# First feed-forward pass of a four-layer kernel: its weights loaded on ScalarE's queue into eleven tiles, split by ScalarE and VectorE; stacks cleared on Pool

## The chip, the cores and the metric

The kernel runs on one core of one Trainium2 chip. Its time is the device time of one execution in microseconds. Several executions are measured, and the median is given; one further execution is profiled. Engines are called TensorE (PE in the profile; PEld is its loading of weights), VectorE (DVE), ScalarE (ACT), Pool (GpSimd, POOL) and SyncE (SP), which issues the transfers.

## The reference, cut to what matters

The program is one chain of four blocks over x of shape (4, 1024, 128), each block a half feed-forward, a mixer and the half feed-forward again. The change touches the first line only:

```python
def _layernorm(x, axis=-1, eps=1e-05):
    m = jnp.mean(x, axis=axis, keepdims=True)
    v = jnp.var(x, axis=axis, keepdims=True)
    return (x - m) / jnp.sqrt(v + eps)
...
    def _L0_ffn_ref(x, w1_w, w1_s, w2_w, w2_s, h1_w, h1_s, h2_w, h2_s, w3_w, w3_s):
        ...
        def _tlin(x, w, s):
            return jnp.einsum('bsi,oi->bso', x, w) * s
        h = jax.nn.silu(_tlin(x, w1_w, w1_s)) * _tlin(x, w2_w, w2_s)
        h = jax.nn.gelu(_tlin(h, h1_w, h1_s), approximate=False)
        h = jax.nn.gelu(_tlin(h, h2_w, h2_s), approximate=False)
        return _tlin(h, w3_w, w3_s)
...
    x = x + 0.5 * _L0_ffn_ref(_layernorm(x, axis=-1), L0_ffn_w1_w, ..., L0_ffn_w3_s)
    x = x + _L0_attn_ref(_layernorm(x, axis=-1), ...)
    x = x + 0.5 * _L0_ffn_ref(_layernorm(x, axis=-1), L0_ffn_w1_w, ..., L0_ffn_w3_s)
    x = x + 0.5 * _L1_ffn_ref(...)
    ...
```

The feed-forward has 128 inputs and 512 hidden features; its weights are 128 x 5632 numbers as the kernel holds them. Attention, two kinds of Mamba mixer, mixtures of experts and a linear attention follow.

## The kernel before

**Layout.** The 4096 tokens stay in SBUF in `x_res`, features on the partitions, as eight chunks of 512 tokens. A feed-forward pass runs over the chunks i = 0 to 7. Products that must be exact to float32 are made of rounded parts: a matrix is split into a high part (rounded to the type fp32r) and a low part (what is left), and `split_mm` (L240 to L243) does three matmuls, high by high, low by high and high by low.

**Order of the work.** Every piece of work is a small generator, such as `dve_stage` or `pe_ffn_gated`, that yields a planned time ahead of each step. `weave` (L86) merges the generators of one engine by these planned times into one fixed list of instructions. On the chip an engine goes through its list in order and stops wherever it has to wait for a semaphore; the planned times set the order and nothing else. `T_FFN` is the planned start of the first hidden layer; all later plans are sums on it.

**The start.** SyncE loads the constants (`sp_setup`, nine transfers, L269 to L277), the chunks of x, and the weights of the first feed-forward in eleven pieces of 128 x 512 through the two tiles of `weight_staging` (`sp_stage`, L464). VectorE (`dve_setup`) waits for all constants, makes the router's two parts and bfloat16 copies, and raises `const_ready`; TensorE, ScalarE and Pool wait for that ahead of their first work. `dve_stage` makes each piece's high part by a cast (L473) and its low part by a subtraction (L475), and frees the staging tile. `dve_attn_setup` clears the stacks of the attention (L771 to L775); SyncE (`sp_attn_setup`) then writes rows of ones into them (L767).

**A chunk.** Its norm: four transposes on TensorE (L355), statistics on VectorE (L364 to L371), a power on Pool (L380), flattening on VectorE (L391), transposes back (L401), the high part on ScalarE (L411) and the low part on VectorE (L428). Four gates follow (f = 0 to 3): two products into PSUM (TensorE, L241 to L243), tanh (ScalarE, L550), two combining steps (VectorE, L559 and L563), high part (ScalarE, L576), low part (VectorE, L585). Then eight hidden tiles (o = 0 to 7): twelve matmuls each, two Gelus on ScalarE (L627, L628) and a low part on VectorE (L637); a last product and the sum into x. The low part of the weights is waited for by count (`wl_lo`): two pieces for the gates, six for the first hidden layer, ten for the second, eleven for the last product.

```python
    T_FFN = 42.0
    w0_count = stage_weights(3.0, 2.4, lambda: (), in_pieces(w0r, w0, L0W_COLS))
...
    on_dve += [dve_attn_setup, dve_ring, dve_found]
```

## Time and profile before

| | us |
|---|---|
| median of 3 runs | 3579.4 (3575.9 to 3581.34) |
| the profiled execution | 3582.58 |
| its span, first to last instruction | 3580.7 |
| TensorE busy | 3103.5 (87%) |
| VectorE busy | 2532.0 (71%) |
| ScalarE busy | 1999.0 (56%) |
| Pool busy | 660.5 (18%) |

The profile is one execution recorded by the hardware. Its page lists the busy time of each engine and of groups of instructions. Its rows name an engine, a line of the kernel, the operation and what it writes and reads. Behind a row or a group stands the idle time of the engine just before it and, after an arrow, what ended it. PEclk is the clock that TensorE was granted, as a share of full speed. SPq rows are transfers that SyncE issues; their time is that of issuing.

### The profile page before, as it was taken

The numbers are of one execution on the slowest core, as the hardware profiler recorded it, in microseconds if no ns is written. First come the engines' busy times: TensorE is split into PE (matmuls) and PEld (weight loads), VectorE is DVE, ScalarE is ACT, GpSimd is POOL, SyncE is SP. The second block draws the span as 40 slices with busy tenths as digits, with TensorE's granted clock in tenths as the row PEclk, the third lists the DMA queues.
The fourth block names the chain that finished last, engine by engine and source line by source line (L and its number), as shares of the span: only waits on it lengthen the run. The fifth ranks groups of instructions, "written<-read, shape, count | busy, mean of one in ns | idle before, by whom it ended". The sixth has DMA issues, their size and how long they took to land. (4 is left out here: it accounts for less than half of the span.)

```text
span 3580.7 us, 45680 instructions
## 1 busy us (share of the span) xinstructions
PE 3103.5 (87%) x15362; PEld 1927.4 (54%) x15362; DVE 2532.0 (71%) x5665; ACT 1999.0 (56%) x3483; POOL 660.5 (18%) x543
## 2 busy tenths in 40 slices
PE   4998888888999997689887777778899999799998
PEld 3776344343677663256543333334467776667776
DVE  5566677774554776778666888876677777667776
ACT  2443566667444444544435565643367777367776
POOL 0011101100000000000003444430023333023332
PEclk8999899999999998889998898889999999799999
DMA  2000122211100330023330000002421010011111
GB/s 83 1 10 28 45 60 64 66 56 35 42 1 1 111 101 2 0 69 97 106 108 27 1 0 1 1 18 86 136 66 43 29 48 27 1 45 42 30 48 51
DMA packets 99184, 159.65 MB, mean 45 GB/s; under 512 B 16220, under 2 KB 28956, under 8 KB 98824
## 3 DMA queue, kind: packets, MB, share of 16 engines
q1 hardware_dynamic: 98952, 156.74, 14.5%
q8 instruction: 123, 2.02, 0.2%
q14 instruction: 109, 0.89, 0.1%
HBM read 138.67 MB, written 17.99 MB: 44 GB/s over the span
## 5 line engine op out<-in xcount | busy, mean ns | idle before, releaser
L380 POOL TENSOR_TENSOR norm_rstd<-norm_rstd,minus_half 128x4 f32<-128x4 f32 x144 | 176.4, 1225 | 1594.3 <-DVE norm_rstd L371 1591.9
L2301 ACT ACTIVATE main_tiles_r<-banks,feature_cols 128x512 fp32r<-128x512 f32 x512 | 352.8, 689 | 188.5 <-PE banks L243 166.7
L2309 DVE TENSOR_TENSOR main_tiles_r<-main_tiles,main_tiles_r 128x512 fp32r<-128x512 f32 x512 | 382.7, 763 | 68.3 <-ACT main_tiles L2302 66.8
L862 DVE TENSOR_REDUCE gate_scratch<-banks 128x2 f32<-128x1024 f32 (+2 forms) x320 | 349.9, 1114 | 106.5 <-PE banks L812 62.7
L241 PE MATMUL banks<-normed_pairs,moe_weights 128*128 128x512 f32 x800 | 407.2, 509 | 13.9 <-ACT main_tiles L2302 6.5
L1010 ACT ACTIVATE main_tiles<-banks 128x512 f32<-128x512 f32 (+3 forms) x768 | 327.3, 497 | 163.2 <-PE banks L232 94.3
L2302 ACT ACTIVATE main_tiles<-banks,feature_cols 128x512 f32<-128x512 f32 x512 | 350.0, 684 | 0.0
L242 PE MATMUL banks<-normed_pairs,moe_weights 128*128 128x512 f32 x800 | 317.4, 397 | 0.0
L243 PE MATMUL banks<-normed_pairs,moe_weights 128*128 128x512 f32 x800 | 317.2, 397 | 0.0
L2346 POOL TENSOR_TENSOR normed<-normed,main_tiles 128x512 f32<-128x512 f32 x128 | 217.6, 1700 | 535.3 <-DVE main_tiles L2335 535.3
L241 PE MATMUL banks<-main_tiles_r,moe_weights 128*128 128x512 f32 x640 | 267.3, 418 | 29.4 <-DVE main_tiles_r L2309 26.9
L243 PE MATMUL banks<-main_tiles_r,moe_weights 128*128 128x512 f32 x640 | 250.9, 392 | 0.0
L242 PE MATMUL banks<-main_tiles_r,moe_weights 128*128 128x512 f32 x640 | 250.6, 392 | 0.0
L241 PE MATMUL banks<-main_tiles_r,ffn_weights 128*128 128x512 f32 x560 | 227.8, 407 | 10.9 <-DVE main_tiles_r L585 6.8
L241 PEld LDWEIGHTS banks<-normed_pairs,moe_weights 128*128 128x128 f32 x800 | 152.6, 191 | 135.9 <-ACT main_tiles L2302 48.9
L243 PE MATMUL banks<-main_tiles_r,ffn_weights 128*128 128x512 f32 x560 | 222.3, 397 | 0.0
L242 PE MATMUL banks<-main_tiles_r,ffn_weights 128*128 128x512 f32 x560 | 222.1, 397 | 0.0
L391 DVE TENSOR_SCALAR norm_flat<-banks,norm_means,norm_rstd 128x128 f32<-128x128 f32 x576 | 195.2, 401 | 29.6 <-POOL norm_rstd L380 29.5
L994 PE MATMUL banks<-q_stacks,k_stacks 64*128 64x512 bf16 (+3 forms) x768 | 179.6, 335 | 39.2 <-ACT main_tiles L1010 37.2
L401 PE MATMUL banks<-const_mats,norm_flat 128*128 128x128 f32 x576 | 104.9, 311 | 103.8 <-DVE norm_flat L391 103.3
L2215 POOL TENSOR_TENSOR mamba_tiles<-mamba_tiles 128x512 f32<-128x512 f32 x128 | 167.3, 1307 | 148.3 <-DVE mamba_tiles L2183 93.6
L364 DVE BATCH_NORM_STATS2 norm_stats<-banks 128x6 f32<-128x128 f32 x576 | 126.9, 282 | 79.0 <-PE banks L355 78.6
(347 smaller groups left out, 6850.0 us busy)
## 6 DMA issues: line engine op xcount, KB each, us to landing
main_tiles<-gates_d SPq DMA_DIRECT2D x400, 256.0 KB, 3.4
weight_staging<-in_w SPq DMA_DIRECT2D x33, 256.0 KB, 3.8
found_d<-main_tiles SPq DMA_DIRECT2D x32, 256.0 KB, 2.0
parts_d<-bf_parts SPq DMA_DIRECT2D x48, 128.0 KB, 1.8
q_stacks<-parts_d SPq DMA_DIRECT2D x192, 32.0 KB
k_stacks<-parts_d SPq DMA_DIRECT2D x192, 32.0 KB
x_res<-in_x_t SPq DMA_DIRECT2D x8, 256.0 KB, 3.4
weight_staging<-found_d SPq DMA_DIRECT2D x8, 256.0 KB, 3.5
```

The lines of the kernel that those rows point to most:

```text
L241: eng.matmul(o, wh, hi, start=first, stop=False)
L242: eng.matmul(o, wl, hi, start=False, stop=False)
L243: return eng.matmul(o, wh, lo, start=False, stop=last)
L380: eng.tensor_tensor(rstd[:, k, 1, :], rstd[:, k, 0, :], minus_half[:, :], ALU.pow).then_inc(s.norm_pow)
L391: z = eng.tensor_scalar(flat[:, k, sl], psum[:, b, sl], means[:, k, t, 0:1], rstd[:, k, 1, t:t + 1], ALU.subtract, ALU.mult)
L862: eng.tensor_reduce(o.rearrange("p (n s) -> p s n", s=2)[:, :, j0:j0 + per], psum[:, b0:b0 + 2, 0:per * (k1 - k0)].rearrange("p s (n c) -> ...
L994: z = eng.matmul(o[:, 0:C - q0], k_of(g, h, i * TILE, (i + 1) * TILE), q_of(g, h, half * C + q0, half * C + C), start=True, stop=not diag, ...
L1010: eng.activation(weight_tile(e)[:, 0:C - q0], psum[:, score_at[e], 0:C - q0], ACT.Exp, scale=HD ** -0.5).then_inc(s.at_exp)
L2301: eng.activation(pair_3(j)[0], psum[:, 2 + j % 2, :], ACT.Relu, bias=bias)
L2302: eng.activation(h3_of(j), psum[:, 2 + j % 2, :], ACT.Relu, bias=bias).then_inc(s.m3_h)
L2309: eng.tensor_tensor(lo, h3_of(j), hi.bitcast(F32), ALU.subtract).then_inc(s.m3_lo)
L2346: eng.tensor_tensor(total, total, gt_of(m3_u(k)), ALU.add).then_inc(s.moe_add)
```

## The change

The first pass no longer goes through the staging tiles. ScalarE issues the eleven loads ahead of everything else, into eleven tiles of `attn3_tiles`, a region that is used much later (the stacks of the attention overlay it). ScalarE makes the high parts with a Copy activation and VectorE the low parts. Four semaphores group the tiles by two, four, four and one. The clearing of the stacks goes to Pool and waits for all low parts, as it shares the place. SyncE issues chunk 0 and the identity first, and TensorE's first transposes wait for these two only (`mats_in`). VectorE's router block stands later. The chunks 2 to 7 share three semaphores, two by two. `T_FFN` goes from 42 to 27. Lines of the changed kernel: transposes L358, statistics L367 to L374, power L383, flattening L394, transposes back L404, norm's high and low part L414 and L431, weights' high and low part L511 and L517, tanh L588, gate steps L597 and L601, gate's high and low part L614 and L623.

```diff
-    x_ready = [lambda c=c: (x_in[c], 16) for c in range(NC_)]
+    x_ready = [lambda c=c: (x_in[c], 16 if c < 2 else 32) for c in range(NC_)]
...
     def sp_setup(eng):
         yield 0.0
+        eng.dma_start(chunk(0), x_t[:, 0:C]).then_inc(x_in[0], 16)
+        eng.dma_start(matf[:, :], mats[:, 0:KEPT_MATS]).then_inc(s.mats_in, 16)
         eng.dma_start(colv[:, :], cols).then_inc(s.const_in, 16)
+        eng.dma_start(chunk(1), x_t[:, C:2 * C]).then_inc(x_in[1], 16)
         eng.dma_start(rowv[:, :], rows).then_inc(s.const_in, 16)
-        eng.dma_start(matf[:, :], mats[:, 0:KEPT_MATS]).then_inc(s.const_in, 16)
...
-        for c in range(NC_):
-            yield 0.1 + (0 if c < 2 else 8 + c)
+        for c in range(2, NC_):
+            yield 16.0 + 8 * (c // 2)
...
     def dve_setup(eng):
...
-        yield 1.0
-        eng.wait_ge(s.const_in, 144)
-        for kind, ne in (("l1", 8), ("l2", 9), ("l3", 8)):
-            w = RW[kind]
-            eng.tensor_copy(routerr[:, 2 * w:2 * w + ne], routerw[:, w:w + ne]).then_inc(s.const_ready)
+        yield 5.5
+        eng.wait_ge(s.mats_in, 16)
+        eng.wait_ge(s.const_in, 128)
         eng.tensor_copy(matb[:, 0:P], ident)
...
+        yield 40.0
         for kind, ne in (("l1", 8), ("l2", 9), ("l3", 8)):
...
     def pe_setup(eng):
         yield 0.0
-        eng.wait_ge(s.const_ready, 6)
...
+        eng.wait_ge(s.mats_in, 16)
+        yield 60.0
+        eng.wait_ge(s.const_ready, 7)
...
-    T_FFN = 42.0
-    w0_count = stage_weights(3.0, 2.4, lambda: (), in_pieces(w0r, w0, L0W_COLS))
+    T_FFN = 27.0
+    w0_pieces = in_pieces(w0r, w0, L0W_COLS)
...
+    def w0_group(k):
+
+        return (0, 2) if k < 2 else (1, 4) if k < 6 else (2, 4) if k < 10 else (3, 1)
+
+    def act_w0_in(eng):
+        yield 0.0
+        for k, (_, src) in enumerate(w0_pieces):
+            eng.dma_start(w0_tile(k), src).then_inc(w0_in[w0_group(k)[0]], 16)
+
+    def w0_at(k):
+        return 6.0 + 1.5 * k
+
+    def act_w0_hi(eng):
+        for k, (dst, _) in enumerate(w0_pieces):
+            yield w0_at(k)
+            n, count = w0_group(k)
+            eng.wait_ge(w0_in[n], 16 * count)
+            eng.activation(dst[:, 0, :], w0_tile(k), ACT.Copy).then_inc(s.w0_hi)
+
+    def dve_w0_lo(eng):
+        for k, (dst, _) in enumerate(w0_pieces):
+            yield w0_at(k) + 0.8
+            eng.wait_ge(s.w0_hi, k + 1)
+            eng.tensor_tensor(dst[:, 1, :], w0_tile(k), dst[:, 0, :].bitcast(F32), ALU.subtract).then_inc(s.w0_lo)
...
     def sp_attn_setup(eng):
-        yield 20.0
+        yield 60.0
...
-    def dve_attn_setup(eng):
-        yield 12.0
+    def pool_attn_clear(eng):
+        yield 34.0
         eng.memset(fin_ones, 1.0)
+        eng.wait_ge(s.w0_lo, len(w0_pieces))
         eng.memset(ks_t.bitcast(F32)[:, :, :, :], 0.0)
-        yield 18.0
+        yield 40.0
         eng.memset(qs_t.bitcast(F32)[:, :, :, :], 0.0)
         eng.memset(v_t[:, :, :], 1.0).then_inc(s.at_set)
```

VectorE's list before, from the low part of the first norm (L428) on; `weight_staging` holds a piece of weights, `ffn_weights` its two parts, and L559, the first gate's combining step, stands nineteen rows below the last one shown:

```order
L428 TENSOR_TENSOR normed_pairs<-banks,normed_pairs 128x512 [waits norm_out]
L473 CAST ffn_weights<-weight_staging 128x512 [waits wl_in0]
L475 TENSOR_TENSOR ffn_weights<-weight_staging,ffn_weights 128x512 [waits wl_hi]
L771 MEMSET gate_scratch 128x1024
L772 MEMSET k_stacks 128x6144
L473 CAST ffn_weights<-weight_staging 128x512 [waits wl_in1]
L475 TENSOR_TENSOR ffn_weights<-weight_staging,ffn_weights 128x512 [waits wl_hi]
L473 CAST ffn_weights<-weight_staging 128x512 [waits wl_in0]
L475 TENSOR_TENSOR ffn_weights<-weight_staging,ffn_weights 128x512 [waits wl_hi]
L774 MEMSET q_stacks 128x3072
L775 MEMSET v_rows 128x1408
L473 CAST ffn_weights<-weight_staging 128x512 [waits wl_in1]
```

VectorE's list in the changed kernel, from behind the flattening of the first norm to the combining step of the first gate (L597):

```order
L517 TENSOR_TENSOR ffn_weights<-attn_tiles,ffn_weights 128x512 [waits w0_hi] x3
L431 TENSOR_TENSOR normed_pairs<-banks,normed_pairs 128x512 [waits norm_out]
L517 TENSOR_TENSOR ffn_weights<-attn_tiles,ffn_weights 128x512 [waits w0_hi]
L367 BN_STATS norm_stats<-banks 128x6 [waits norm_in]
L367 BN_STATS norm_stats<-banks 128x6 x3
L371 BN_AGGR norm_means<-norm_stats 128x2 [waits norm_stat]
L371 BN_AGGR norm_means<-norm_stats 128x2 x3
L374 TENSOR_SCALAR norm_rstd<-norm_means 128x4 [waits norm_mean]
L517 TENSOR_TENSOR ffn_weights<-attn_tiles,ffn_weights 128x512 [waits w0_hi] x3
L394 TENSOR_SCALAR norm_flat<-banks,norm_means,norm_rstd 128x128 [waits norm_pow]
L394 TENSOR_SCALAR norm_flat<-banks,norm_means,norm_rstd 128x128 x3
L597 SCALAR_TENSOR_TENSOR spare_nat<-spare_nat,banks 128x512 [waits ffn_tanh]
```

The clearing and the casts are gone from between the two, and seven of the eleven subtractions are left there. Right behind it, VectorE's list of the changed kernel in the first two gates:

```order
L601 SCALAR_TENSOR_TENSOR spare_nat<-banks,half_s_and_half_s_s_63,spare_nat 128x512 [waits ffn_mid,ffn_gt]
L517 TENSOR_TENSOR ffn_weights<-attn_tiles,ffn_weights 128x512 [waits w0_hi] x2
L623 TENSOR_TENSOR main_tiles_r<-spare_nat,main_tiles_r 128x512 [waits ffn_ghi]
L431 TENSOR_TENSOR normed_pairs<-banks,normed_pairs 128x512 [waits norm_out]
L597 SCALAR_TENSOR_TENSOR spare_nat<-spare_nat,banks 128x512 [waits ffn_tanh]
L601 SCALAR_TENSOR_TENSOR spare_nat<-banks,half_s_and_half_s_s_63,spare_nat 128x512 [waits ffn_mid,ffn_gt]
L517 TENSOR_TENSOR ffn_weights<-attn_tiles,ffn_weights 128x512 [waits w0_hi] x2
L623 TENSOR_TENSOR main_tiles_r<-spare_nat,main_tiles_r 128x512 [waits ffn_ghi]
```

Four subtractions stand in the gates, where before none stood. ScalarE's list before, from its start:

```order
L411 ACT_TABLE_LOAD [waits norm_back]
L411 ACTIVATE normed_pairs<-banks 128x512 [waits const_ready]
L550 ACTIVATE spare_nat<-banks,half_s_and_half_s_s_63 128x512 [waits ffn_up]
L576 ACTIVATE main_tiles_r<-spare_nat 128x512 [waits ffn_g]
L411 ACTIVATE normed_pairs<-banks 128x512 [waits norm_back]
```

And now; `attn_tiles` is where the eleven pieces land:

```order
L501 DMA attn_tiles<-in_w 128x512 x11
L511 ACT_TABLE_LOAD
L511 ACTIVATE ffn_weights<-attn_tiles 128x512 [waits w0_in0] x2
L414 ACTIVATE normed_pairs<-banks 128x512 [waits norm_back]
L511 ACTIVATE ffn_weights<-attn_tiles 128x512 [waits w0_in1] x4
L511 ACTIVATE ffn_weights<-attn_tiles 128x512 [waits w0_in2]
L588 ACTIVATE spare_nat<-banks,half_s_and_half_s_s_63 128x512 [waits const_ready,ffn_up]
L511 ACTIVATE ffn_weights<-attn_tiles 128x512 [waits w0_in2] x2
L614 ACTIVATE main_tiles_r<-spare_nat 128x512 [waits ffn_g]
```

The table load stands ahead of the first copy and no longer behind the first norm; a copy of the third group (`w0_in2`) stands ahead of the first tanh (L588). TensorE's list keeps its order but for two places some hundreds of microseconds later, where two neighbours change places.

## Rows read from the trace of the kernel before

**Rows 1.** Waits, 0 to 80 us: who waited for whom, us in total, times, longest

```profile
ACT main_tiles_r L576 <- DVE spare_nat L563: 34.4, 4, 29.3
...
DVE ffn_weights L473 <- DMA weight_staging<-in_w: 6.4, 3, 4.3
```

**Rows 2.** Order of time, VectorE, 21 to 50 us: start us, us, engine, line, operation

```profile
21.48 5.18 DVE L772 MEMSET k_stacks<- 128x6144 f32 x1 [1.23 <-issue]
...
42.77 0.43 DVE L473 CAST ffn_weights<-weight_staging 128x512 fp32r<-128x512 f32 x1 [4.33 <-DMA weight_staging<-in_w]
...
49.02 0.68 DVE L559 SCALAR_TENSOR_TENSOR spare_nat<-spare_nat,banks 128x512 f32<-128x512 f32 x1
```

**Rows 3.** Order of time, 7 to 21 us, constants to the first tanh

```profile
7.37 0.32 DVE L292 CAST router_w_r<-router_w 128x8 fp32r<-128x8 f32 x3 [6.29 <-DMA main_tiles<-in_mats]
...
8.35 0.31 DVE L301 TENSOR_TENSOR router_w_r<-router_w,router_w_r 128x8 fp32r<-128x8 f32 x3
...
8.99 1.11 PE L355 MATMUL banks<-const_mats,x_res 128*128 128x128 f32 x4 [8.99 <-DVE half_s_and_half_s_s L306]
...
11.80 1.05 POOL L380 TENSOR_TENSOR norm_rstd<-norm_rstd,minus_half 128x4 f32<-128x4 f32 x1 [11.36 <-DVE norm_rstd L371]
...
12.88 1.36 DVE L391 TENSOR_SCALAR norm_flat<-banks,norm_means,norm_rstd 128x128 f32<-128x128 f32 x4 [0.18 <-POOL norm_rstd L380]
...
15.50 1.28 ACT L411 ACT_TABLE_LOAD   x1 [15.50 <-PE banks L401]
...
17.42 0.69 DVE L428 TENSOR_TENSOR normed_pairs<-banks,normed_pairs 128x512 fp32r<-128x512 f32 x1 [2.12 <-ACT normed_pairs L411]
...
18.17 1.12 PE L355 MATMUL banks<-const_mats,x_res 128*128 128x128 f32 x4 [2.75 <-DVE normed_pairs L428]
...
20.60 0.69 ACT L550 ACTIVATE spare_nat<-banks,half_s_and_half_s_s 128x512 f32<-128x512 f32 x1 [3.21 <-PE banks L243]
```

**Rows 4.** Stretch 20 to 48 us: length, busy us by engine, PEclk, DMA share, GB/s

```profile
20.00:48.00 28.00, 1.85 (x5) 0.93 (x3) 19.18 (x30) 0.69 (x1) 1.12 (x1) 0.59 0.43 146
```

**Rows 5.** Order of time, a gate's low part and the first hidden matmul

```profile
54.73 0.69 DVE L585 TENSOR_TENSOR main_tiles_r<-spare_nat,main_tiles_r 128x512 fp32r<-128x512 f32 x1 [0.70 <-ACT main_tiles_r L576]
...
61.19 0.50 PE L241 MATMUL banks<-main_tiles_r,ffn_weights 128*128 128x512 f32 x1 [3.28 <-DVE main_tiles_r L585]
```

**Rows 6.** Order of time, SyncE's issues of the last constant and of chunks 0, 1

```profile
4.96 0.60 SPq L277 DMA_DIRECT2D main_tiles<-in_mats  x1
5.60 1.06 SPq L280 DMA_DIRECT2D x_res<-in_x_t  x2
```

**Rows 7.** Stretches of 3 us, columns as in rows 4

```profile
6.00:9.00 3.00, 0.01 (x1) 0.02 (x1) 1.52 (x13) 0.00 (x0) 0.00 (x0) 1.00 0.79 195
...
36.00:39.00 3.00, 0.00 (x0) 0.00 (x0) 1.12 (x2) 0.00 (x0) 0.00 (x0) 0.50 1.02 410
```

**Rows 8.** Groups, 0 to 62 us: line, engine, shapes, count, busy us, mean ns, idle before

```profile
L475 DVE TENSOR_TENSOR ffn_weights<-weight_staging,ffn_weights 128x512 fp32r<-128x512 f32 x11 | 7.6, 692 | 0.4
...
L576 ACT ACTIVATE main_tiles_r<-spare_nat 128x512 fp32r<-128x512 f32 x4 | 2.5, 630 | 34.4 <-DVE spare_nat L563 34.4
```

**Rows 9.** Order of time, TensorE at the sixth gate's first product

```profile
76.69 0.50 PE L241 MATMUL banks<-normed_pairs,ffn_weights 128*128 128x512 f32 x1 [1.32 <-DVE spare_nat L559]
```

**Rows 10.** Groups, Pool, whole run: its memset of the odd v rows

```profile
L1096 POOL MEMSET v_rows_odd<- 128x1408 f32 x1 | 1.3, 1271 | 0.0
```

**Rows 11.** TensorE's clock: a stretch (columns as in rows 4), the page's 40 slices

```profile
62.00:66.10 4.10, 4.10 (x13) 3.19 (x12) 0.00 (x0) 0.64 (x2) 0.00 (x0) 0.58 0.00 0
...
PEclk8999899999999998889998898889999999799999
```

**Rows 12.** Order of time, Pool and VectorE subtract at once, 250 to 253 us

```profile
250.75 1.66 POOL L887 TENSOR_TENSOR spare_nat<-spare_nat 128x512 f32<-128x512 f32 x1 [1.73 <-DVE spare_nat L839]
251.19 1.77 DVE L637 TENSOR_TENSOR main_tiles_r<-spare_a,main_tiles_r 128x512 fp32r<-128x512 f32 x1
```

More of the change, by code:

```diff
@@ L482, in build, with w0_tile @@
     FFN_US = 31.0
-    T_FFN = 42.0
-    w0_count = stage_weights(3.0, 2.4, lambda: (), in_pieces(w0r, w0, L0W_COLS))
+    T_FFN = 27.0
+    w0_pieces = in_pieces(w0r, w0, L0W_COLS)
+    def w0_tile(k):
+        return wb_t[:, k, :]
+    def w0_group(k):
[17 more added lines that the diff above has]
+            eng.tensor_tensor(dst[:, 1, :], w0_tile(k), dst[:, 0, :].bitcast(F32), ALU.subtract).then_inc(s.w0_lo)
+    on_act += [act_w0_in, act_w0_hi]
+    on_dve.append(dve_w0_lo)
     ffn_b = [T_FFN + FFN_US * i for i in range(NC_)]
@@ L529, in pe_ffn_gated @@
                 if i == 0 and f == 0:
-                    eng.wait_ge(s.wl_lo, 2)
+                    eng.wait_ge(s.w0_lo, 2)
                 if q == 32:
@@ L547, in act_ffn_tanh @@
                 eng.wait_ge(s.ffn_up, q + 1)
+                if q == 0:
+                    eng.wait_ge(s.const_ready, 3)
                 if q >= 2:
```

47 lines of the change are left out of this document (24 added, 23 removed).

## The prediction

> **What bounds the kernel now.** I read the list of waits of the first 80 us first, since every edit of the change lies there. The reader is to see one wait that is out of proportion: ScalarE's rounding of the first gate tile (L576) waits 34.4 us for VectorE in four times, 29.3 us of it in one, while the weights' own transfers cost VectorE only 6.4 us [rows 1]. Next VectorE's part of the order of time. The tanh of the first gate is started at 20.60, so its tile is ready at 21.3, but VectorE takes it up (L559) only at 49.02. In between stand, in one in-order queue, the clearing of the k stacks (5.18 us in one instruction), of the q stacks and v rows, eight of the eleven weight splits, some of which wait for a transfer (4.33 us at 42.77), and the second norm [rows 2, 3]. The table of stretches gives the whole gap: from 20 to 48 us VectorE is busy for 19.18 us of 28, TensorE for 1.85 [rows 4]. So the first gate of the first feed-forward pass, and with it all that TensorE has to do later, waits for VectorE's queue, and not for data. From 61 us on the kernel runs as a chain of semaphores in which TensorE is busy for most of the time, and nothing in it goes by the clock on the wall: what is won before the first hidden layer (first matmul at 61.19) [rows 5] is won for the end, unless something gives it back.
>
> **The change, part by part: the start.** What stays on the path are the constants, the norms of chunk 0 and 1, the splits that stand ahead of the first gate, and the four gates. I rebuild the times from rows.
> 1. TensorE now waits for chunk 0 and the identity only, SyncE's first two transfers. Before, its first transposes waited for all constants and start at 8.99 [rows 3]. They can now start at about 6 (0.6 MB and as much of weights, 3 us at the fast rate, after those 2.5), but VectorE does its constant casts ahead of the flattening (L394 of the new kernel), and these still wait for the last constant. Call that landing T. Before it ends the wait at 7.37; SyncE's last constant was issued from 4.96 to 5.56, so it took 1.8 us more [rows 3, 6]. SyncE now issues two chunks ahead of it at 0.53 us each (1.06 for two) [rows 6], which puts T at 8.4 at the earliest. At the latest: SyncE's list up to there is 1.4 MB (two chunks 0.5, the matrices 0.35 and 0.2, the rest small), and ScalarE's queue may bring as much again of weights beside it. 2.8 MB at the slow row's 195 GB/s are 14.4 us, at the fast row's 410 GB/s 6.8 us, and some 2.5 us from the first issue to the first landing come on top: 17 or 9.3 [rows 7]. The slow stretch held the many small constants, and what is added are pieces of 256 KB, so I stay near the fast end: **T = 10.5**, with 8.4 and 17 as ends.
> 2. VectorE's constant block takes 1.6 us before (7.37 to 8.99); its six router instructions, 0.32 and 0.31 us [rows 3], go to a later place. It ends at T + 1.0 = 11.5. The first norm's power is done by then (2.8 us from the transposes to Pool's start, and 1.05 us: 6 + 3.9 = 9.9) [rows 3].
> 3. From flattening to the paired residue (L428) it was 12.88 to 17.42, 4.54 us, with a table load of 1.28 in it [rows 3]. The table load now stands ahead of ScalarE's weight copies, beside the transfers: 3.2 us are left. New in between are one weight copy on ScalarE and one subtraction on VectorE (the third tile's; order section), 0.63 and 0.69 us [rows 8]. L428's work starts at 11.5 + 3.2 + 1.3 = 16.0.
> 4. The second transposes follow 0.75 us later (18.17 against 17.42), the tanh 2.4 us after these (20.60), Pool's power 2.8 us after them and 1.05 us long [rows 3]: 16.8, 19.2, 19.6 to 20.7. VectorE does three more subtractions (2.1 us) from 19.6, then the flattening of 1.36 us [rows 3, 8], and takes up the first gate at **23.0 where it was 49.02**.
> 5. The four gates took 61.19 − 49.02 = 12.17 us before [rows 2, 5]. Four subtractions of 0.69 now stand in them, two and two, each pair in a gap in which VectorE waited 0.70 us for ScalarE's rounding [rows 5, 8]: + 2 × (1.38 − 0.70) = 1.4. First hidden matmul at 23.0 + 12.2 + 1.4 = **36.5 where it was 61.19**. Gained: 24.7.
>
> **What moves behind it.** The router block (1.0 us with its semaphore) now stands between VectorE's fourth hidden residue and the fifth gate, where TensorE already waits 1.32 us for VectorE [rows 9]: − 1.0, and 0 if it is hidden. ScalarE's eleven casts cost 11 × 0.63 = 6.9 us [rows 8] in a stretch in which it waited 34 us [rows 1]; its eleven DMA issues some 5 us by SyncE's 0.53, over at about 6 and ahead of anything it must do. Eleven casts (L473) leave VectorE. The clearing goes to Pool, at 0.90 ns an element by Pool's own memset (1271 ns for 1408) [rows 10]: k stacks 5.5, q stacks 2.8, v rows 1.3, together 9.6 us, begun when the last split is done, at about 29. It is over by 39; Pool's next power was needed at 83 and is now needed at 59, and the stacks are wanted only by the attention, hundreds of microseconds later. So it costs nothing unless it holds VectorE (first rival). SyncE loses nine waits on staging and issues chunks 2 to 7, the rope table and the attention weights at once. The rest of the program keeps its order but for two places on TensorE where neighbours change; I put these at nothing. The two staging tiles change their turn only.
>
> **The sum.** 24.7 − 1.0 = 23.7 us. The profiled execution took 3582.58 (span 3580.7, 1.9 around it), so it would be 3558.9. That execution lay 3.2 above the median of the runs, 3579.4, so I forecast **3555.7**.
>
> **What would speed it up.** T at 8.4 (−2.1), the four subtractions hidden (−1.4), the router block hidden (−1.0), and the slow piece of the first hidden layer gone: 62 to 66.1 has a granted clock of 0.58, between the levels 1.2 and 2.4 GHz, so 42% of 4.1 us, 1.7, were lost [rows 11]. Together −6.2: 3549.5.
>
> **Rivals.**
> *Transfers come late.* For it: 5.2 MB (ten weight tiles, and as much on SyncE's list) are wanted by about 20 us, and the stretch 6 to 9 moved 195 GB/s at a busy share of 0.79 [rows 7]. Against: 36 to 39 moved 410 GB/s from SyncE's queue alone. Price: T at 17 is + 6.5. ScalarE's seventh copy needs tiles 6 to 9 by 20.2 (one copy of 0.63 ahead of the third subtraction after 19.6) and stands ahead of the tanh; 5.2 MB at 410 GB/s are there at 15, at 195 GB/s at 29.2, + 9, and the two do not add. 3559 to 3565.
> The Trainium skill (DMA: Bandwidth & Descriptors, Issuing engines are not separate DMA queues) speaks against the change here: starting DMAs from several engines saves only the time of issuing. By it the second queue brings no bandwidth and T lies between 9.3 and 17; if the queues' rates added up, T would be 8.4. No row of this case has two queues at once.
> *Pool's clearing holds VectorE.* For it: while Pool subtracts at 250.75 (1.66 us), VectorE's subtraction with two SBUF inputs takes 1.77 us in place of 0.69 [rows 8, 12]. If a memset did the same, the residues of the second and third gate would stand behind 5.5 us, then 2.8 and 1.3: + 5 to + 9.6, 3561 to 3565. Against: that Pool instruction reads SBUF, a memset only writes; the row shows no such case.
> The Trainium skill (SBUF — State Buffer, Who interferes with whom) says that a VectorE instruction with two SBUF inputs contends with a GpSimd one that reads SBUF, not with one that only writes. By that the price is 0, by the row's slowdown carried over up to 9.6; no run here shows it yet.
> *The clock takes it back: slower than before.* The profile shows TensorE at a lowered clock after a stretch with gaps: 0.58 at 62 to 66.1, and the page's row of the clock has 11 slices of 40 below 9 tenths, spread over the run [rows 11]. All of them fall anew when the work starts 24 us earlier. At half clock and full work a microsecond costs half of one: to lose the 23.7 and 7.2 more (0.2%) the run needs 62 us more of half clock, fifteen pieces like that one. From there on it is slower, 3587. Against: the three runs before differ by 5.4 us in all, though their pieces fell as they liked. Taking back half of that spread is likely, all of the gain is not.
> *The change does not move the wait.* VectorE would still reach the first gate behind its queue. The order section excludes it: seven subtractions stand ahead of it, no memset and no wait on a staging tile.
>
> **Chances.** The forecast (3550 to 3559) 0.68, late transfers 0.15, Pool holding VectorE 0.07, more gain than 3549.5 0.04, the clock taking most or all back 0.04, no move 0.02. The range 3549 to 3565 holds the first three and leaves out about 1 in 10. About 0.2%, 7.2 us, is what a measurement of this kernel can tell from no change. Faster by more: 0.95; within it: 0.03; slower by more: 0.02.
>
> **What the new profile would show.** Right: VectorE's first gate step at 22 to 24 and the first hidden matmul at 35 to 38; the wait of ScalarE's rounding for VectorE down from 29.3 to a few us; Pool's memsets from 29 to 39 with VectorE's subtractions at 0.69 beside them; all later landmarks some 24 us earlier up to the end. Wrong: VectorE's constant casts starting after 13 (late transfers); a subtraction of 2 us or more beside a memset (Pool); the hidden layer 24 us earlier but the end less than 18 (the clock, or a wait that I have not seen behind the first pass).

## The result, and the profile after

The changed kernel takes 3559.44 us (median of four runs, 3552.9 to 3562.62) against 3580.37 of the kernel before (3575.9 to 3583.12): a ratio of 0.994 with a 95% interval of 0.9922 to 0.9958, 15 to 28 us. Forecast were 3555.7 in a range of 3549 to 3565. The profiled execution took 3557.94 (span 3555.8). In a second series of the same kernel (first experiment below) the ratio is 0.9931, interval 0.9914 to 0.9948.

First the waits of the first 60 us, which answer to [rows 1] (who waited for whom, us in total, times, longest). ScalarE's rounding of the gates (now L614) waited 34.4 us for VectorE before; one wait of 29.3 is gone. VectorE's wait for the last constant, 6.29 us at the very start before [rows 3], now stands behind the statistics of the first norm, from 8.87 to 14.16.

```profile
ACT main_tiles_r L614 <- DVE spare_nat L601: 9.1, 5, 3.1
...
DVE const_mats_bf L294 <- DMA main_tiles<-in_mats: 5.3, 1, 5.3
```

The order of time from the first transposes to the fifth gate, which answers to [rows 2, 3, 5, 9] (start us, us, engine, line, operation). The landmarks are the constant casts (L294), the flattening (L394), the paired residue (L431), the first tanh (L588), VectorE's first gate step (L597), and TensorE at the first hidden matmul and at the matmul of [rows 9], which waits for VectorE's first step of the fifth gate; below it stands for "the fifth gate".

```profile
6.20 1.11 PE L358 MATMUL banks<-const_mats,x_res 128*128 128x128 f32 x4 [6.20 <-DMA const_mats<-in_mats]
...
9.02 1.01 POOL L383 TENSOR_TENSOR norm_rstd<-norm_rstd,minus_half 128x4 f32<-128x4 f32 x1 [8.57 <-DVE norm_rstd L374]
...
14.16 0.23 DVE L294 CAST const_mats_bf<-const_mats 128x128 bf16<-128x128 f32 x1 [5.29 <-DMA main_tiles<-in_mats]
...
15.18 1.36 DVE L394 TENSOR_SCALAR norm_flat<-banks,norm_means,norm_rstd 128x128 f32<-128x128 f32 x4
...
19.51 0.68 DVE L431 TENSOR_TENSOR normed_pairs<-banks,normed_pairs 128x512 fp32r<-128x512 f32 x1
...
22.68 0.69 ACT L588 ACTIVATE spare_nat<-banks,half_s_and_half_s_s 128x512 f32<-128x512 f32 x1 [1.74 <-PE banks L244]
...
25.90 0.68 DVE L597 SCALAR_TENSOR_TENSOR spare_nat<-spare_nat,banks 128x512 f32<-128x512 f32 x1
...
32.56 5.23 POOL L811 MEMSET k_stacks<- 128x6144 f32 x1 [7.29 <-DVE ffn_weights L517]
...
35.66 0.69 DVE L623 TENSOR_TENSOR main_tiles_r<-spare_nat,main_tiles_r 128x512 fp32r<-128x512 f32 x1 [0.70 <-ACT main_tiles_r L614]
...
39.25 0.80 PE L242 MATMUL banks<-main_tiles_r,ffn_weights 128*128 128x512 f32 x1 [3.27 <-DVE main_tiles_r L623]
...
56.29 0.50 PE L242 MATMUL banks<-normed_pairs,ffn_weights 128*128 128x512 f32 x1 [1.91 <-DVE spare_nat L597]
```

VectorE reaches the first gate at 25.90 where it was 49.02, and TensorE the hidden layer at 39.25 where it was 61.19: 21.9 us earlier. At the fifth gate the lead is 76.69 − 56.29 = 20.4. Pool clears beside VectorE's subtraction, which takes its 0.69.

The stretches, which answer to [rows 4, 7, 11] (length, busy us and count of PE, PEld, DVE, ACT, POOL, then PEclk, DMA share, GB/s). In the fast stretch of [rows 7] one queue moved 410 GB/s; here two queues together move 352 to 368 from 3 to 12 us, at a busy share of about 1. Two rows from the list of queues for 0 to 13 us stand behind them (packets, MB, share of 16 engines): q10 is ScalarE's, q1 SyncE's.

```profile
3.00:6.00 3.00, 0.00 (x0) 0.00 (x0) 0.00 (x0) 0.00 (x0) 0.00 (x0) 1.00 0.99 352
6.00:9.00 3.00, 1.11 (x4) 0.71 (x4) 1.44 (x9) 1.74 (x2) 0.00 (x0) 1.00 1.03 368
9.00:12.00 3.00, 0.00 (x0) 0.00 (x0) 0.00 (x0) 0.70 (x2) 1.01 (x1) 1.00 1.08 353
...
20.00:48.00 28.00, 20.48 (x59) 14.24 (x60) 16.99 (x36) 11.49 (x19) 11.33 (x5) 0.76 0.08 32
```

```profile
q10 hardware_dynamic: 1249, 2.29, 51.9%
q1 hardware_dynamic: 1328, 1.48, 35.4%
```

From 20 to 48 us TensorE is now busy for 20.48 of 28 us; it was 1.85. The last rows are the rest of the run behind the same matmul, at 82.5 us before and 62.1 after; the third is an experiment that comes below (late splits). First before, then after, then the experiment:

```profile
82.50:3580.70 3498.20, 3070.39 (x15243) 1903.10 (x15241) 2487.01 (x5570) 1981.72 (x3458) 658.17 (x537) 0.95 0.15 44
```

```profile
62.10:3555.80 3493.70, 3069.98 (x15243) 1901.08 (x15241) 2486.83 (x5570) 1981.93 (x3458) 658.52 (x537) 0.95 0.14 44
```

```profile
55.40:3559.80 3504.40, 3082.68 (x15243) 1907.48 (x15241) 2485.41 (x5570) 1983.64 (x3458) 658.49 (x537) 0.94 0.14 43
```

With the same number of instructions the rest takes 3498.2, 3493.7 and 3504.4 us. So the lead of 20.4 at the fifth gate became 24.9 at the end in this execution. On the way it went down to 14.5, at the matmul that started at 1852 us before. Both traces have the same 15362 matmuls, in the same order but for neighbours at two places, so they can be matched one by one. I cut them behind the fifth gate into 255 stretches of 60 matmuls. In 227 of these TensorE's time at a lowered clock is the same in both traces within 0.3 us, and they move the lead by −0.15 us in all; the other 28 move it by +4.6. So the gain behind the fifth gate goes with where the lowered clock fell, and not with what the change did to the work there.

### The profile page after: what moved, and what is told of

Read it like the earlier page. It is cut to its first block and busy times, and to the rows that moved or that the text cites. A ratio compares the mean times of both kernels' runs of the same rounds, so it can differ in the third digit from the quotient of the medians.

```text
span 3555.8 us, 45680 instructions
## 1 busy us (share of the span) xinstructions
PE 3104.9 (87%) x15362; PEld 1926.3 (54%) x15362; DVE 2517.0 (71%) x5650; ACT 2005.2 (56%) x3494; POOL 671.1 (19%) x547
## 5 line engine op out<-in xcount | busy, mean ns | idle before, releaser
L383 POOL TENSOR_TENSOR norm_rstd<-norm_rstd,minus_half 128x4 f32<-128x4 f32 x144 | 176.4, 1225 | 1555.9 <-DVE norm_rstd L374 1553.5
L901 DVE TENSOR_REDUCE gate_scratch<-banks 128x2 f32<-128x1024 f32 (+2 forms) x320 | 349.9, 1115 | 110.4 <-PE banks L851 62.1
L242 PEld LDWEIGHTS banks<-normed_pairs,moe_weights 128*128 128x128 f32 x800 | 153.2, 191 | 132.9 <-ACT main_tiles L2341 48.6
L394 DVE TENSOR_SCALAR norm_flat<-banks,norm_means,norm_rstd 128x128 f32<-128x128 f32 x576 | 195.3, 402 | 29.4 <-POOL norm_rstd L383 29.3
L367 DVE BATCH_NORM_STATS2 norm_stats<-banks 128x6 f32<-128x128 f32 x576 | 127.1, 283 | 84.0 <-PE banks L358 83.8
L243 PEld LDWEIGHTS banks<-normed_pairs,moe_weights 128*128 128x128 f32 x800 | 153.6, 192 | 56.5 <-issue 40.9
```

Source lines behind the costliest of these rows:

```text
L242: eng.matmul(o, wh, hi, start=first, stop=False)
L243: eng.matmul(o, wl, hi, start=False, stop=False)
L383: eng.tensor_tensor(rstd[:, k, 1, :], rstd[:, k, 0, :], minus_half[:, :], ALU.pow).then_inc(s.norm_pow)
L394: z = eng.tensor_scalar(flat[:, k, sl], psum[:, b, sl], means[:, k, t, 0:1], rstd[:, k, 1, t:t + 1], ALU.subtract, ALU.mult)
L901: eng.tensor_reduce(o.rearrange("p (n s) -> p s n", s=2)[:, :, j0:j0 + per], psum[:, b0:b0 + 2, 0:per * (k1 - k0)].rearrange("p s (n c) -> ...
```

## The experiments

Theory one is that of the prediction, with one term corrected: the gain is the time by which VectorE's queue reaches the first gate earlier; the last constant came 3.7 us later than forecast, because the weights on ScalarE's queue took transfer bandwidth from it. The rivals: the queues share nothing and SyncE's own pace sets the landing; Pool's clearing costs; something behind the first pass takes or gives the rest.

This table holds the landmarks of every kernel's trace: start of the constant casts, VectorE's first gate step, TensorE's first hidden matmul, and how much earlier than before (61.19, 76.69, 3580.7) come this matmul, the one at the fifth gate and the last instruction of the span.

```
kernel                    casts  first gate  hidden   earlier at:  hidden  fifth gate  end    ratio to before (95%)
before                     7.60     49.02    61.19                   -        -         -     1
the change                14.16     25.90    39.25                 21.9     20.4      24.9    0.994  (0.9922 to 0.9958)
  again                   14.16     25.92    39.27                 21.9     21.3      22.2    0.9931 (0.9914 to 0.9948)
  casts late              49.91     21.16    34.11                 27.1     24.8      26.5    0.9923 (0.9902 to 0.9944)
  casts and splits late   32.85     20.55    32.99                 28.2     27.1      20.9    0.9925 (0.9908 to 0.9941)
  three tiles first       11.29     23.04    36.38                 24.8     24.3      23.6    0.9942 (0.9923 to 0.9961)
  one queue               16.41     28.15    41.50                 19.7     18.2      23.8    one run, 3559.05
  splits on VectorE       14.15     27.90    42.10                 19.1     18.6      18.1    one run, 3564.67
  Pool reads to clear     14.71     26.45    40.58                 20.6     19.3      17.8    one run, 3564.66
  clearing on VectorE     14.41     26.15    39.54                 21.7     14.9      14.8    0.9958 (0.9942 to 0.9973)
before, Pool clears        7.73     44.65    56.77                  4.4      4.4       4.6    0.9987 (0.9972 to 1.0001)
before, Pool, ScalarE      7.67     40.49    52.69                  8.5      8.6       6.7    one run, 3576.1
```

**The change again.** The unchanged kernel, beside the first three experiments on their chip.

> The changed kernel once more, unaltered, to see what of its time moves by itself. The first look put its first hidden matmul at 39.25 us, 21.9 us earlier than before, but the end 24.9 us earlier; in between the lead went down to 16.2 and up again in steps of about 1.5 us. Theory one (the steps are TensorE's clock, whose lowered pieces fall differently in every execution): again 39.2 +- 0.5 at the first hidden matmul, but steps of 1 to 2 us at other places behind it, and an end anywhere in 3553 to 3563. Theory two (the change itself moves later work): the same steps at the same places, within 0.5 us, and an end within 1 us of 3557.9.

Measured: 3556.17 (3548.73 to 3572.63, eight runs) against 3582.22. Every landmark up to the hidden layer agrees within 0.02 us with the first trace, the lead at the fifth gate is 21.3 and not 20.4, and at the end 22.2 and not 24.9. What lies behind the start moves the end by several microseconds, as theory one has it. The start itself repeats well but not always to 0.02: in three other kernels with the same transfer lists the constant casts start at 14.15, 14.41 and 14.71.

**The constant casts behind the first gates.**

```
-        eng.dma_start(colv[:, :], cols).then_inc(s.const_in, 16)
+        eng.dma_start(colv[:, :], cols).then_inc(s.cols_in, 16)
...
-        eng.wait_ge(s.mats_in, 16)
-        eng.wait_ge(s.const_in, 128)
-        eng.tensor_copy(matb[:, 0:P], ident)
...
+        eng.wait_ge(s.cols_in, 16)
...
+        eng.wait_ge(s.mats_in, 16)
+        eng.wait_ge(s.const_in, 112)
+        eng.tensor_copy(matb[:, 0:P], ident)
...
```

> The changed kernel, but VectorE's four bfloat16 casts of constants stand 35 us later in the plan, beside the router block; ahead of the first flattening it waits for the column constants only, which have a semaphore of their own. Theory one (the late landing of the last constant, at 14.16, sets the start): flattening at about 10.1, when Pool's power ends, in place of 15.18, and everything up to the first hidden matmul 5 us earlier, 34.2 in place of 39.25; the end 4 to 5 us earlier than the changed kernel. Rival (weights' tiles are next in line, since they come over the same saturated transfers: tiles 2 to 5 by 12, tiles 6 to 9 by 17): flattening at 10.1 but the first gate's step only 2 to 3 us earlier, 36.5 at the first hidden matmul. Rival two (the casts cost the same where they are now, between hidden residues and the fifth gate): 1 us is given back behind 45 us.

VectorE's first gate step and TensorE's first hidden matmul in this kernel:

```profile
21.16 0.68 DVE L598 SCALAR_TENSOR_TENSOR spare_nat<-spare_nat,banks 128x512 f32<-128x512 f32 x1
```

```profile
34.11 0.80 PE L242 MATMUL banks<-main_tiles_r,ffn_weights 128*128 128x512 f32 x1 [3.19 <-DVE main_tiles_r L624]
```

The wait for the last constant was worth 5.1 us at the hidden layer. Nothing else on the path needs those constants yet. At 49.91, ahead of the fifth gate, the moved casts and a piece of lowered clock (0.77 from 52 to 59.3 us) take back 2.3 of the lead over the change (0.7 and 1.6), and 2.8 are left behind that gate; the time, 3555.67, can't be told from the change's.

**Three weight tiles first.** ScalarE issues three tiles at the start and eight behind its first two copies. This asks directly what set the landing of the constants.

```
         for k, (_, src) in enumerate(w0_pieces):
+            if k == 3:
+                yield 7.6
             eng.dma_start(w0_tile(k), src).then_inc(w0_in[w0_group(k)[0]], 16)
```

> The change with ScalarE issuing three weight tiles at the start and the other eight only behind its first two copies; nothing else moves. It tests the mis-sized term of the prediction, the landing of the last constant (10.5 forecast, 14.16 measured in the change). Theory one (the weight tiles take the bandwidth from the constants: 350 GB/s in all, and more than half of it to ScalarE's queue): ahead of the last constant stand SyncE's 1.4 MB and three tiles of 256 KB, 2.2 MB, at 350 GB/s 6.3 us behind the first landing at about 3 us: VectorE's constant casts start at 9.3 to 11, the flattening at 10.3 to 12. The first gate step comes at 22 to 23 in place of 25.9 unless a later weight tile is late: tiles 3 to 10 (2.1 MB) are issued behind the copies and have landed at 17 to 19. Rival (SyncE's pace of issuing and the landing of small constants set it): the casts still start at 13 or later and the first gate step comes at 25 or later. The end: 3554 to 3560, of which the clock decides the half.

VectorE's constant casts and its first gate step:

```profile
11.29 0.23 DVE L294 CAST const_mats_bf<-const_mats 128x128 bf16<-128x128 f32 x1 [2.26 <-DMA main_tiles<-in_mats]
...
23.04 0.67 DVE L599 SCALAR_TENSOR_TENSOR spare_nat<-spare_nat,banks 128x512 f32<-128x512 f32 x1
```

The casts start 2.87 us earlier, the first gate step 2.86, the hidden layer 2.87. 11.29 is a little later than the 9.3 to 11 I expected (ScalarE issues tiles again from 6.63 on, so more than three stood ahead of it), and far from the rival's 13. SyncE's list and its pace are unchanged, so the weights on the other queue did hold up the constants. The time, 3557.93, shows none of the 2.9 us. The trace shows where the first 1.6 went: a piece of lowered clock, 0.77, fell on the fifth gate, where the change had 1.00. First this kernel, then the change, whose stretch opens 0.8 us ahead of the gate (columns as in the stretches above):

```profile
52.40:59.80 7.40, 7.39 (x27) 5.75 (x28) 3.56 (x8) 3.05 (x6) 0.00 (x0) 0.77 0.00 0
```

```profile
55.50:62.10 6.60, 5.81 (x27) 4.60 (x28) 4.30 (x11) 3.06 (x6) 0.00 (x0) 1.00 0.00 0
```

The same 27 matmuls keep TensorE busy for 7.39 us in place of 5.81, and the lead over the change falls from 3.9 at that gate to 2.3 behind it.

**One queue.** SyncE issues the weight tiles too, one behind each of its first transfers.

```
+        w0_next()
         eng.dma_start(chunk(0), x_t[:, 0:C]).then_inc(x_in[0], 16)
+        w0_next()
         eng.dma_start(matf[:, :], mats[:, 0:KEPT_MATS]).then_inc(s.mats_in, 16)
...
-    on_act += [act_w0_in, act_w0_hi]
+    on_act += [act_w0_hi]
```

> The changed kernel, but SyncE issues the eleven weight loads too, one after each of its own transfers, so all 22 come from one queue. Theory one (the transfers are saturated, 350 to 390 GB/s at a busy share of 1 from 3 to 22 us in the change, and a second queue only shares that out): the last constant lands at 13 to 15 as in the change (14.16), first hidden matmul within 1.5 us of 39.3. Rival (one queue issues too slowly: 0.46 to 0.6 us each, 20 issues until the last constant, 10.5 us, and moves less): the last constant lands at 15 to 17 and the end of the chunk loads moves by the same, first hidden matmul 2 to 3 us later, rate below 300 GB/s.

```profile
16.41 0.23 DVE L309 CAST const_mats_bf<-const_mats 128x128 bf16<-128x128 f32 x1 [5.99 <-DMA main_tiles<-in_mats]
```

The casts start 2.25 us later than with two queues, the gate and the hidden layer follow by the same 2.25. Both numbers lie where the rival had them (landing at 15 to 17, hidden layer 2 to 3 us later), and outside theory one's (13 to 15, within 1.5). Against the 14.71 of the kernel with Pool's reads, measured beside this one, it is 1.7. So the time of issuing counts: SyncE issues the last constant at 10.76 in place of 6.46, and one queue moved 265 GB/s from 3 to 6 us, where two moved 352. The rival's low rate held no longer than that: 324 against 368 from 6 to 9, and 363 against 353 from 9 to 12. The Trainium skill (DMA: Bandwidth & Descriptors, Issuing engines are not separate DMA queues) says that issuing from several engines saves issuing time alone. The traces agree: 2.25 us, and from 9 us on no higher rate with two queues than with one.

**Pool's clearing alone.** The kernel before with the clearing on Pool, nothing else.

```
-    on_dve += [dve_attn_setup, dve_ring, dve_found]
+    on_dve += [dve_ring, dve_found]
-    on_pool += [pool_turned, pool_found, pool_attn_setup]
+    on_pool += [pool_attn_clear, pool_turned, pool_found, pool_attn_setup]
```

> The kernel before, and of the change only one part: the stacks are cleared by Pool, at the planned time at which VectorE did it. Weights still come through the two staging tiles. Theory one (the staging by two tiles is then the bound: a piece takes about 0.4 of issue, 2.9 of transfer and 1.1 of splitting, two in flight, 2.3 us each for eight pieces behind 19 us): VectorE's first gate step at about 39 in place of 49.02, gain 10 us. Rival (the clearing was the whole hold-up, transfers keep up with VectorE): first gate step at about 30, gain 19 us, and the new way of the weights is worth almost nothing. Rival two (Pool's power of the second norm, behind the clearing, becomes late): first gate step later than 40, gain under 8.

3576.6 (3567.86 to 3583.9, ten runs), which is not told from no change by the interval, and 4.4 us at the hidden layer, where 9.0 us of memsets (k stacks, q stacks and v rows) had left VectorE. The first gate step comes at 44.65 and not at the expected 39. Pool's memset and VectorE's cast beside it:

```profile
13.82 5.21 POOL L772 MEMSET k_stacks<- 128x6144 f32 x1
```

```profile
14.30 5.02 DVE L473 CAST ffn_weights<-weight_staging 128x512 fp32r<-128x512 f32 x1
19.35 0.69 DVE L475 TENSOR_TENSOR ffn_weights<-weight_staging,ffn_weights 128x512 fp32r<-128x512 f32 x1
20.56 1.64 DVE L473 CAST ffn_weights<-weight_staging 128x512 fp32r<-128x512 f32 x1
```

The cast of 0.41 us ([rows 8] have the splits' group) is held for 5.02: it ends at 19.32, 0.29 us behind the memset's end at 19.03. The next two casts, beside the memsets of the q stacks and the v rows, take 1.64 and 0.78, and these two memsets 2.93 and 1.54 us, where they take 2.66 and 1.27 in the change. So the clearing did hold VectorE, in an instruction that I had not thought of: the cast, and not the subtraction.

**Pool's clearing and ScalarE's copies.** The same, with the high parts of the splits on ScalarE, so that no cast is left beside Pool.

```
-            eng.tensor_copy(hi, tile).then_inc(s.wl_hi)
+            if k >= 11:
+                eng.tensor_copy(hi, tile).then_inc(s.wl_hi)
...
+            eng.activation(dst[:, 0, :], staging_tile(k, src)[0], ACT.Copy).then_inc(s.wl_hi)
```

> The kernel before with the clearing on Pool and the high parts of the first pass's weights made by ScalarE (Copy), still through the two staging tiles. In the run with the clearing alone VectorE's second cast took 5.02 us beside Pool's memset of 5.21, and the next two 1.64 and 0.78. Theory one (that cast was held by the memset, because a VectorE copy from SBUF to SBUF and Pool's write want the same port): no instruction of VectorE above 1.4 us in the first 60 us, the first gate step 5 to 6 us earlier than there (44.65), so at 38 to 40. Rival (the cast waited for its transfer and the profile shows it as length): VectorE shows a wait of 4 to 5 us for the second piece, first gate step within 1.5 us of 44.65.

No VectorE instruction is stretched, and the first gate step comes 4.2 us earlier than in the experiment before, at 40.49 (expected 38 to 40). With the same list of transfers ScalarE's copy of the second piece starts at 12.46, so the piece is there well before 14.30, when the held cast began: the cast did not wait for its transfer. What holds the start now are the two staging tiles in turn:

```profile
33.30 1.27 ACT L482 ACTIVATE ffn_weights<-weight_staging 128x512 fp32r<-128x512 f32 x2 [4.97 <-DMA weight_staging<-in_w]
```

From here to the change's 25.90 are 14.6 of the 23.1 us gained at this landmark. By subtraction they belong to the eleven tiles loaded at once, and to the order that this allows; the earlier first norm is no part of it, since the first flattening starts at 13.27 here and at 15.18 in the change. No run has the tiles alone.

**The weights alone.** The change with the clearing on VectorE.

```
-    on_dve += [dve_ring, dve_found]
+    on_dve += [dve_attn_clear, dve_ring, dve_found]
-    on_pool += [pool_attn_clear, pool_turned, pool_found, pool_attn_setup]
+    on_pool += [pool_turned, pool_found, pool_attn_setup]
```

> The changed kernel, but VectorE clears the stacks, at the planned time at which Pool does in the change, behind the last split; so the other part of the change alone. Theory one (VectorE has room between the hidden residues, but a clearing of 5.2 us in one piece is longer than a gap of 2): first hidden matmul as in the change, 39.3, then TensorE held for 2 to 6 us in the first hidden layer, end 2 to 6 us later than the changed kernel. Rival (it lands inside the gates and stands ahead of one): first hidden matmul at 44 or later, end 8 to 9 us later. Rival two (gaps take it all): no difference above 1 us.

The lead is still 21.7 at the hidden layer, since the memsets now stand behind it, and falls to 13.6 behind the fifth gate, for which VectorE comes late:

```profile
48.13 5.18 DVE L811 MEMSET k_stacks<- 128x6144 f32 x1 [1.23 <-issue]
...
57.11 2.62 DVE L813 MEMSET q_stacks<- 128x3072 f32 x1 [0.59 <-issue]
...
61.12 0.63 DVE L597 SCALAR_TENSOR_TENSOR spare_nat<-spare_nat,banks 128x512 f32<-128x512 f32 x1
```

3568.39 is 12.2 us more than the unchanged kernel's 3556.17 beside it, where 2 to 6 were expected; the intervals of the two ratios just overlap. In the trace 6.8 to 7.7 of it are there by 69 us (13.6 against leads of 20.4 and 21.3); where the rest comes from, or whether it is scatter, no run shows. So the change is not "load the weights at once" alone: a third of its lead in the trace comes with the clearing on Pool.

**Pool reads to clear.** The change with the k and q stacks cleared by subtracting chunk 1 from itself, so that Pool reads SBUF.

```
-        eng.memset(ks_t.bitcast(F32)[:, :, :, :], 0.0)
+                eng.tensor_tensor(ks_t.bitcast(F32)[:, n, m, :], chunk(1), chunk(1), ALU.subtract)
```

> The changed kernel, but Pool clears the k and q stacks by subtracting a chunk of x from itself, eighteen instructions of 128 x 512 that read SBUF, in place of two memsets. Theory one (what matters to VectorE's two-input subtractions is whether Pool reads): subtractions of VectorE that fall beside Pool's take 1.1 to 1.8 us in place of 0.69, and Pool's own are stretched to 1.3 to 1.7; first hidden matmul 1 to 3 us later than 39.3. Rival (the reading makes no difference, VectorE is only held by copies and casts, as in the run with the clearing alone, where a cast beside Pool's memset took 5.02 us): subtractions stay at 0.69, hidden matmul at 39.3.

```profile
33.12 13.29 POOL L814 TENSOR_TENSOR k_stacks<-x_res 128x512 f32<-128x512 f32 x12 [7.30 <-DVE ffn_weights L517]
```

```profile
39.23 1.29 DVE L623 TENSOR_TENSOR main_tiles_r<-spare_nat,main_tiles_r 128x512 fp32r<-128x512 f32 x1 [0.69 <-ACT main_tiles_r L614]
```

VectorE's subtractions with two SBUF inputs take 0.88 and 1.29 us beside it (1.38 and 1.11 later), against 0.69 beside a memset. A fifth, at 47.31, keeps its 0.69; Pool's next instruction begins 0.06 us behind it and takes 1.53 in place of 1.03. So reading is what matters for them, and who began first, though 1.38 is milder than the 1.77 of [rows 12]. Of the 1.3 us by which the hidden layer comes later, 0.8 are these subtractions; 0.55 stand already at the constant casts.

**Splits on VectorE.** The change with `eng.tensor_copy` on VectorE for the eleven high parts, in place of ScalarE's copies.

> The change with the high parts of the eleven weight tiles cast by VectorE (as in the kernel before) and not by ScalarE; transfers, tiles and Pool's clearing stay. Theory one (VectorE's queue bounds the start; each cast moved off it is worth its 0.42 us where VectorE does not wait): five casts now stand ahead of the first gate and four in the gates, the first gate step comes 1.5 to 2.5 us later (27.5 to 28.5), the first hidden matmul 2.5 to 4 us later (42 to 43), and ScalarE's rounding waits as much longer for VectorE. Rival (VectorE waits for landings anyway, the casts are hidden): the first gate step within 0.5 us of 25.9 and the first hidden matmul within 1 us of 39.25. End: 3556 to 3564, the look alone can't tell it.

```profile
24.58 1.07 DVE L511 CAST ffn_weights<-attn_tiles 128x512 fp32r<-128x512 f32 x1
...
27.90 0.68 DVE L597 SCALAR_TENSOR_TENSOR spare_nat<-spare_nat,banks 128x512 f32<-128x512 f32 x1
```

The first gate step comes 2.0 us later and the hidden layer 2.9: theory one, for VectorE's queue is the bound up to there. The expectation counted five casts ahead of the gate; eight stand there (3.4 us and more), and part of them fell into waits. One of the eight took 1.07 us beside Pool's memset of the gate scratch (24.42, 0.95 us long), a further case of a held cast.

**Casts and late splits out of the way.** The casts late as above, and with them the router block and five of the subtractions, moved into the gap between the fourth gate and the first hidden residue, where VectorE waits for ScalarE.

```
-        yield 40.0
+        yield 28.8
...
-        return 6.0 + 1.5 * k
+        return 6.0 + 1.5 * k if k < 6 else 28.2 + 0.3 * (k - 6)
```

> The changed kernel with VectorE's constant casts and router block, and the splits of tiles 6 to 10 on ScalarE and VectorE, moved into the gap between the fourth gate and the first hidden residue, in which VectorE waits 6.9 us and ScalarE 5.0 us; flattening waits for the column constants only. Theory (the start is VectorE's queue and nothing else; four subtractions in the gates cost 1.4 us, the router block 0.6, the casts 5 by their wait): first hidden matmul at 32.4 where the changed kernel has 39.25 and the run with late casts 34.0, and no loss at the fifth gate, so a lead over the kernel before of 28 us at 62 us, end 6 to 8 us earlier than the changed kernel give or take 3 by the clock. Rival (casts and five subtractions, 4.9 us, don't fit the gap, or Pool's clearing, which now begins about 38, collides with them or comes late for the third norm): lead at 62 us not above 25. Tells apart: lead at 62 us.

The hidden layer starts at 32.99, and at the fifth gate the lead is 27.1, the largest of all. At the end 20.9 are left. The third of the three rows on the rest of the run has it: the same 15243 matmuls are busy for 3082.68 us, 12.7 more than in the change, at a mean clock of 0.94 in place of 0.95. I added up the time under a lowered clock behind that point from the trace's record: 371 us before, 367 in the change, 398 here. Over the eleven traces of changed kernels, what the end gained or lost beyond the lead at that point goes with that sum (correlation −0.84, about 0.22 us lost for each microsecond). Matched matmul by matmul with the kernel before, as in the section on the result, the 229 stretches of 60 matmuls with the same clock move this kernel's lead by +1.3 us, the other 26 by −7.5. That is a correlation; no run here sets the clock.

## Why the prediction came out as it did

- **What bounds the kernel**: right. The queue of VectorE ahead of the first gate was the bound, and what was won there reached the end within the few microseconds that the clock moves it.
- **Step 1, the last constant**: this is the term that was mis-sized. T was forecast at 10.5 and is 14.16, within my ends of 8.4 and 17 but past the mark of 13 that I had named for late transfers. The step let ScalarE's queue bring "as much again" as SyncE's; by 13 us it had brought 2.29 MB to 1.48. 3.77 MB by 13 us fit 350 GB/s and a start of the transfers at some 2.2 us, and the fast row's 410 was not reached. TensorE's first transposes start at 6.20, forecast about 6. With three tiles first T is 11.29, and the first gate (23.04, forecast 23.0) and the hidden layer (36.38, forecast 36.5) come where the prediction had them; that is in part luck, as T is still 0.8 late there and steps 3 and 4 are 0.8 shorter than forecast.
- **Step 2**: right (1.02 us from T to the flattening; forecast 1.0).
- **Steps 3 and 4**: 10.7 us from the flattening to the first gate, forecast 11.5. The paired residue starts 4.3 behind the flattening, forecast 4.5, and the gate 6.4 behind that, forecast 7.0: three subtractions in a row take 1.89 us and not 2.1, and start 0.3 earlier.
- **Step 5**: 39.25 − 25.90 = 13.35, forecast 13.5. So 21.9 were gained at the hidden layer, not 24.7; 22 to 24 for the first gate and 35 to 38 for the hidden layer were missed through T alone.
- **The router block**: TensorE waits 1.91 us where it waited 1.32, so 0.6 was lost, not 1.0. But the lead there is 20.4, so 1.5 were lost since the hidden layer began. The rest, 1.0, is the clock: the first hidden matmul takes 0.80 us in place of the 0.50 of [rows 5], as the clock is 0.50 from 39.25 to 44.55, while before it is lowered only from 62.7 on; by the sixteenth hidden matmul (45.38 against 66.33) the lead has fallen from 21.9 to 20.9. In the second trace of the change this piece falls later, the first hidden matmul takes 0.50, and the lead at the fifth gate is 21.3, so the 0.6 are all that is lost there. The prediction had forecast the slow piece to stay or to go, not to move.
- **ScalarE's part**: eleven copies of 0.621 us (6.9 forecast, 6.1 with overlaps), its issues 6.49 us and not 5; neither is waited for on the path.
- **Late transfers**, the rival: true in part, at 3.7 of its 6.5 us. Its second half (a tile late for ScalarE's seventh copy) did not come: the last packet of ScalarE's queue ends at 16.9 us, so all eleven tiles are there 3.4 us ahead of the seventh copy (20.3). What still moves 423 GB/s from 18 to 21 us is SyncE's queue.
- **Pool holds VectorE**, the rival: not in the change. The subtraction at 35.66 takes 0.69 beside the memset. Pool clears from 32.56 to 41.60, forecast 29 to 39: it begins later by what T was late, and takes 9.2 us and not 9.6. The Trainium skill (SBUF — State Buffer, Who interferes with whom) excludes the case for a subtraction, and the run with reading on Pool agrees (0.88 to 1.38 for four of five). It also names casts, which the change has taken off VectorE; for them the traces agree too, at 5.02 us beside a memset of 5.21 and 1.07 beside one of 0.95. The clearing alone, costed at its 9.0 us of memsets, brings 4.4.
- **The clock**: not slower, but it decides the last microseconds. The gain at the end spans 20.9 to 26.5 us in kernels that lead by 20 to 27 at the fifth gate, in another order. The prediction's price of half a microsecond for each at a lowered clock is that of full work: the piece on the fifth gate of "three tiles first" cost 1.6 us for its 3.4; over the whole run it is about 0.22. The profiled 3557.94 lies 1.0 below the sum's 3558.9 because some 4.5 us won behind the fifth gate, where the clock fell otherwise than before, covered a shortfall of 3.3 (23.7 forecast, 20.4 there, 1.0 of it itself the clock): the sum hit by two errors, and that is luck. The medians can't tell: they give 20.9 us and, in the second series, 26.0, on both sides of 23.7.
- **A better version** exists at the start (casts late, or late splits: 5 to 6 us earlier at the hidden layer), but at the end their ratios, 0.9923 and 0.9925, lie inside the change's two intervals. Whether they are faster stays open; with this spread it would take many more runs.

## What to carry to other kernels

When an in-order queue holds work that nobody waits for ahead of work that somebody does, count the gain at the first thing that waited, and check it there in the trace before reading the end. When a change sends large transfers from a second queue at once, size the landing of the small, urgent ones by the total in flight at the measured rate; sending fewer large ones first gave back 2.9 of the 3.7 us at the casts, though the end doesn't show it. Moving a memset to Pool cost nothing here beside subtractions and reads from PSUM, but much beside a cast from SBUF to SBUF.

## What the runs showed of the hardware

- A VectorE cast from SBUF to SBUF, 0.41 us by itself, took 5.02 us beside a Pool memset of 5.21 that had begun 0.48 us before it. Pool memsets beside later casts took 2.93 and 1.54 us, against 2.66 and 1.27 without.
- A VectorE subtraction with two SBUF inputs keeps its 0.69 us beside a memset, and takes 0.88 to 1.38 beside Pool subtractions that read SBUF, in four of five cases. In the fifth VectorE began 0.06 us ahead of Pool's next instruction: it kept its 0.69, and Pool's took 1.53 us in place of 1.03.
- Two queues together moved 352 to 368 GB/s from 3 to 12 us at a busy share of 0.99 to 1.08. Of the 3.77 MB moved by 13 us 61% were those of the queue that had only pieces of 256 KB; the other had the small constants among its own.
- The same program's time ranges over 3548.7 to 3572.6 us; in the traces, pieces of lowered clock of a few microseconds fall in other places from one execution to the next, and move the end by up to 6 us either way. A piece of 3.4 us on matmuls without a gap cost 1.6 us.
